# Two buffers for each load, three for the gate and x1 + b2, and new orders and banks in a batched graph-attention kernel

## The reference

```python
x = layernorm(x + elu(A(x)))           # layer A: one head, width 256
h = elu(B(x) + b1)                     # layer B: 4 heads of width 128
x = layernorm(x + C(h) + b2)           # layer C: one head, width 256, input width 512
# a layer: V = in @ W; e = leaky_relu(V a1 + (V a2)^T, 0.2), masked by adj;
#          out = softmax(e) @ V
# A masks by adj (softmax over columns), B and C by adj or the diagonal (over rows)
```

## Time and profile before

| | us |
|---|---|
| median of 3 runs | 724.78 (724.01 to 726.85) |
| the profiled execution | 722.46 |
| its span, first to last instruction | 720.7 |
| PE busy | 650.2 (90%) |
| DVE busy | 603.4 (84%) |
| ACT busy | 484.5 (67%) |
| POOL busy | 450.3 (62%) |
| mean granted TensorE clock, share of full | 0.972 |

### The profile page before, as it was taken

The page is one execution under the profiler, slowest core; times in us unless marked ns, Lnnn a source line. Parts: engine busy times, 40 slices in busy tenths (PEclk is TensorE's granted clock), DMA queues, the critical chain, the costliest instruction groups (busy, mean ns, idle before and its releaser), DMA issues. The chain is left out here.

```text
span 720.7 us, 17574 instructions
## 1 busy us (share of the span) xinstructions
PE 650.2 (90%) x4104; PEld 569.4 (79%) x4104; DVE 603.4 (84%) x2368; ACT 484.5 (67%) x1219; POOL 450.3 (62%) x810
## 2 busy tenths in 40 slices
PE   2478999999999999999899999999999999999883
PEld 1367788888888888888788888888888888888772
DVE  3566789989988989988889999899999889888862
ACT  1245777776777777787677776777777777777551
POOL 0215666766667766766667666666677666666752
PEclk9588999999999999999999999999999999999996
DMA  7211112322232213222232223222222123222111
GB/s 216 68 38 59 53 40 95 97 89 67 96 97 95 71 64 97 96 89 67 96 96 81 68 82 96 88 69 96 96 96 89 62 79 94 71 88 67 53 37 44
DMA packets 56085, 58.41 MB, mean 81 GB/s; under 512 B 3760, under 2 KB 51504, under 8 KB 55984
## 3 DMA queue, kind: packets, MB, share of 16 engines
q1 hardware_dynamic: 53152, 55.06, 23.7%
q10 hardware_dynamic: 2832, 2.23, 1.0%
HBM read 36.31 MB, written 8.39 MB: 62 GB/s over the span
## 5 line engine op out<-in xcount | busy, mean ns | idle before, releaser
L346 POOL TENSOR_SCALAR probB<-probB,rdenB 128x256 f32<-128x256 f32 x256 | 119.2, 478 | 101.9 <-DVE rdenB L654 97.8
L428 ACT ACTIVATE probB<-probB,shiftB 128x256 f32<-128x256 f32 x256 | 127.4, 500 | 66.8 <-DVE probB L637 54.1
L873 PE MATMUL PS<-probTB,VB 128*128 128x256 f32 x512 | 126.9, 389 | 0.0
L637 DVE SCALAR_TENSOR_TENSOR probB<-PS,VB,gatedB 128x256 f32<-128x256 f32 x256 | 110.6, 474 | 0.3 <-issue 0.2
L873 PEld LDWEIGHTS PS<-probTB,VB 128*128 128x128 f32 x512 | 91.1, 193 | 17.3 <-ACT probTB L439 8.5
L357 POOL TENSOR_TENSOR inlC<-hidT,inhC 128x512 fp32r<-128x512 f32 x64 | 82.1, 1283 | 24.7 <-ACT inhC L484 24.7
L595 DVE CUSTOM_DVE_ANT_0 gatedB<-PS,gateB 128x256 f32<-128x256 f32 x256 | 93.6, 421 | 2.8 <-issue 0.3
L814 PE MATMUL PS<-WA,xTin 128*128 128x258 f32 x256 | 65.8, 401 | 21.4 <-DMA xTin<-in_x_t_dram 21.2
L329 POOL TENSOR_TENSOR y<-y,xres 128x512 f32<-128x512 f32 x32 | 41.0, 1282 | 69.7 <-DVE y L659 69.7
L829 PE MATMUL PS<-WhB,inhB 128*128 128x260 f32 x256 | 78.2, 305 | 7.0 <-DVE inlB L668 7.0
L829 PE MATMUL PS<-WhC,inhC 128*128 128x258 f32 x256 | 78.1, 305 | 1.0 <-ACT VA L418 1.0
(11 more groups left out here) (98 smaller groups left out, 1651.4 us busy)
## 6 DMA issues: line engine op xcount, KB each, us to landing
adj_in<-in_adj_dram SPq DMA_DIRECT2D x32, 256.0 KB, 3.0
xTin<-in_x_t_dram SPq DMA_DIRECT2D x32, 256.0 KB, 3.7
xres<-in_x_dram SPq DMA_DIRECT2D x32, 256.0 KB, 3.2
adjT_in<-in_adj_t_dram SPq DMA_DIRECT2D x32, 256.0 KB, 2.9
x1c<-x1b SPq DMA_DIRECT2D x32, 256.0 KB, 2.3
out_dram<-res SPq DMA_DIRECT2D x32, 256.0 KB, 2.1
gateC<-gateB SPq DMA_DIRECT2D x32, 128.0 KB, 2.0
WB<-in_L_gnn_W_dram ACTq DMA_DIRECT2D x2, 256.0 KB, 5.8
```

The costliest lines, as they stand in the source:

```text
L346: last = pool.tensor_scalar(B.prob[h][:, k, :], B.prob[h][:, k, :], B.rden[:, k, h:h + 1], 1.0, ALU.mult, ALU.mult)
L428: last = nc.scalar.activation(L.prob[h][:, k, :], L.prob[h][:, k, :], ACT.Exp, bias=L.shift[:, k, h:h + 1], accum_out=den[:, k, h:h + 1] i ...
L637: last = nc.vector.scalar_tensor_tensor(out=L.prob[h][:, k, :], in0=PS[b][:, (h % 2) * N:(h % 2 + 1) * N], scalar=L.V[:, k, h, 1:2], in1=L ...
L873: last = nc.tensor.matmul(PS[b][:, o:o + N], B.V[:, k, h, 2:B.F + 2], B.probT[h][:, k, :], start=(k == 0), stop=(k == NT - 1))
```

## The change

- xTin, xres, adj_in and adjT_in have two buffers and two semaphores each. Batch b uses buffer b % 2, and its load waits for the reader of batch b - 2. All four are issued an iteration ahead of before, in the order residual, transposed adjacency, xT, adjacency, store.
- gate_to_c and x1_to_c are gone. Gate B/C and x1b have three buffers (b % 3), read in place by B and C; make_gate_b waits for the maxima of B and C of batch b - 3, keep_x1 for norm_last of batch b - 3.
- Each engine's list has a new order, over batches t0 to t5 (37 iterations; the first only issues loads). PSUM banks are dealt out anew: the eight-bank table is replaced by a record, kept while the program is built, of what last ended in a bank (take_bank).

The arithmetic is the same. The core of the diff (removed orders stand in the kernel above):

```diff
+    def loaded(self):
+        return (self.at // 2 + 1) * DMA
...
+        xTin = [sb(f"xTin{i}", [P, A.KT, N]) for i in range(2)]
...
+        gate_bc = [sb(f"gate_bc{i}", [P, NT, N], BF16) for i in range(3)]
...
+        x1b = [sb(f"x1b{i}", [P, NT, D]) for i in range(3)]
...
-            for i in range(NB + 4):
+            for i in range(NB + 5):
...
             def load_residual(t):
                 if active(t):
-                    if t.later:
-                        sp.wait_ge(s_t0, t.last())
-                    sp.dma_start(xres[:, :, :], x_v[t.at]).then_inc(s_xr, DMA)
+                    if t.at >= 2:
+                        sp.wait_ge(s_t0, t.this() - 2)
+                    sp.dma_start(xres[t.at % 2][:, :, :], x_v[t.at]).then_inc(s_xr[t.at % 2], DMA)
...
             def body(i):      # sync queue
+                load_residual(t0)
+                load_adjT(t1)
+                load_xT(t0)
+                load_adj(t0)
+                store(t5)
...
             def body(i):      # GpSimd
+                low_c(1, t4)
+                low_c(0, t4)
+                scale(2, t3)
+                scale(3, t3)
+                residual(t2)
+                scale(0, t3)
+                rstd(A, t2)
+                normalise(A, t2)
+                diagonal(t2)
+                fix_scores(t4)
+                scale(1, t3)
+                rstd(C, t5)
+                normalise(C, t5)
+                keep_x1(t2)
...
             def body(i):      # ScalarE
+                high_b(5, t3)
+                elu_exp(1, 0, t4)
+                exp(A, 0, t2)
+                exp(C, 0, t5)
+                weights_copy(B, 1, 2, t4)
+                weights_copy(A, 0, 7, t2)
+                high_c(1, t4)
+                elu_exp(0, 6, t4)
+                weights_copy(C, 0, 3, t5)
+                high_c(0, t4)
+                exp(B, 2, t3)
+                norm_first(1, 3, t2)
+                exp(B, 3, t3)
+                norm_first(0, 5, t2)
+                elu_exp_first(t2)
+                values(A, 1, 7, t1)
+                values(A, 0, 1, t1)
+                exp(B, 0, t3)
+                values(C, 1, 7, t4)
+                weights_copy(B, 2, 3, t3)
+                values(C, 0, 1, t4)
+                exp(B, 1, t3)
+                weights_copy(B, 3, 3, t3)
+                weights_copy(B, 0, 2, t3)
...
             def body(i):      # VectorE
+                make_gate_a(t1)
+                maxima(B, 2, 1, t3)
+                maxima(B, 3, 1, t3)
+                logit(B, 2, 1, t3)
+                elu(0, 6, t4)
+                top(B, 1, t3)
+                values_b(1, 0, 2, t3)
+                shift(B, 1, t3)
+                values_b(0, 0, 0, t3)
+                inverse_sum(A, 1, 3, t2)
+                logit(B, 3, 1, t3)
+                inverse_sum(A, 0, 5, t2)
+                inverse_sum_head(2, t3)
+                maxima(B, 0, 4, t3)
+                maxima(B, 1, 4, t3)
+                inverse_sum_head(3, t3)
+                top(B, 0, t3)
+                logit(B, 0, 4, t3)
+                inverse_sum(C, 1, 2, t5)
+                elu_first(t2)
+                shift(B, 0, t3)
+                norm_last(1, 2, t5)
+                logit(B, 1, 4, t3)
+                inverse_sum_head(0, t3)
+                stats(A, t2)
+                meanvar(A, t2)
+                inverse_sum(C, 0, 0, t5)
+                norm_last(0, 0, t5)
+                maxima(A, 0, 6, t1)
+                stats(C, t5)
+                logit(A, 0, 6, t1)
+                top(A, 0, t1)
+                maxima(C, 0, 4, t4)
+                top(C, 0, t4)
+                meanvar(C, t5)
+                shift(C, 0, t4)
+                shift(A, 0, t1)
+                inverse_sum_head(1, t3)
+                low_b(5, t2)
+                make_gate_b(t1)
+                logit(C, 0, 4, t4)
+                values_b(0, 1, 5, t2)
+                values_b(1, 1, 1, t2)
+                elu(1, 0, t3)
...
             def body(i):      # TensorE
+                project(B, 0, 1, 5, t3)
+                project(B, 1, 1, 1, t3)
+                transpose_weights(B, 1, 2, t4)
+                transpose_weights(A, 0, 7, t2)
+                spread(B, 1, 1, t3)
+                transpose_weights(C, 0, 3, t5)
+                weigh_head(1, 6, t4)
+                project(B, 1, 0, 2, t3)
+                project(B, 0, 0, 0, t3)
+                weigh(A, 1, 3, t2)
+                weigh(A, 0, 5, t2)
+                spread(B, 0, 4, t3)
+                weigh(C, 1, 2, t5)
+                project_a(1, 7, t1)
+                project_a(0, 1, t1)
+                weigh(C, 0, 0, t5)
+                transpose_weights(B, 2, 3, t3)
+                spread(A, 0, 6, t1)
+                project(C, 1, 0, 7, t4)
+                project(C, 0, 0, 1, t4)
+                transpose_weights(B, 3, 3, t3)
+                transpose_weights(B, 0, 2, t3)
+                spread(C, 0, 4, t4)
+                weigh_head(2, 0, t3)
+                transpose_x1(5, t2)
+                weigh_head(3, 0, t3)
+                weigh_head(0, 6, t3)
```

More of the change, by code:

```diff
@@ L327, in residual @@
                     pool.wait_ge(s_y0, t.this())
-                    pool.wait_ge(s_xr, t.this(DMA))
-                    pool.tensor_tensor(y0[:, :, :], y0[:, :, :], xres[:, :, :], ALU.add).then_inc(s_t0, 1)
+                    pool.wait_ge(s_xr[t.at % 2], t.loaded())
+                    pool.tensor_tensor(y0[:, :, :], y0[:, :, :], xres[t.at % 2][:, :, :], ALU.add).then_inc(s_t0, 1)
             def keep_x1(t):
@@ L335, in keep_x1 @@
                     pool.wait_ge(A.s_ln, t.this())
-                    if t.later:
-                        pool.wait_ge(s_x2c, t.last(DMA))
-                    pool.tensor_tensor(x1b[:, :, :], x1[:, :, :], b2p[:, :].unsqueeze(1).to_broadcast([P, NT, D]),
-                                       ALU.add).then_inc(s_x1b, 1)
+                    if t.at >= 3:
+                        for s in C.s_norm:
+                            pool.wait_ge(s, t.this() - 3)
+                    pool.tensor_tensor(x1b[t.at % 3][:, :, :], x1[:, :, :],
+                                       b2p[:, :].unsqueeze(1).to_broadcast([P, NT, D]), ALU.add).then_inc(s_x1b, 1)
             def scale(h, t):
@@ L370, in body @@
             def body(i):
-                t0, t1, t2, t3, t4 = i.batch(0), i.batch(1), i.batch(2), i.batch(3), i.batch(4)
-                residual(t0)
-                scale(3, t1)
-                scale(0, t1)
-                scale(1, t1)
-                rstd(A, t0)
-                fix_scores(t2)
-                keep_x1(t1)
-                normalise(A, t0)
-                rstd(C, t3)
-                normalise(C, t3)
-                diagonal(t0)
-                low_c(1, t1)
-                low_c(0, t1)
-                scale(2, t0)
+                t0, t1, t2, t3, t4, t5 = i.batch(0), i.batch(1), i.batch(2), i.batch(3), i.batch(4), i.batch(5)
+                low_c(1, t4)
[12 more added lines that the diff above has]
+                keep_x1(t2)
             iterations(body)
@@ L698, in norm_last @@
                     dve.wait_ge(C.s_den[u], t.this())
-                    dve.wait_ge(s_x2c, t.this(DMA))
+                    dve.wait_ge(s_x1b, t.this())
                     if t.later:
@@ L729, in body @@
             def body(i):
-                t0, t1, t2, t3, t4 = i.batch(0), i.batch(1), i.batch(2), i.batch(3), i.batch(4)
-                maxima(B, 2, 0, t2)
-                maxima(B, 3, 0, t2)
-                logit(B, 2, 0, t2)
-                top(B, 1, t2)
-                values_b(1, 0, 5, t2)
-                if t2.first:
-                    finish_b2(5)
-                shift(B, 1, t2)
-                inverse_sum(A, 1, 1, t1)
-                logit(B, 3, 0, t2)
-                gate_a(t0)
@@ L742, in body @@
-                inverse_sum(A, 0, 3, t1)
-                inverse_sum_head(2, t2)
-                maxima(B, 0, 6, t2)
-                maxima(B, 1, 6, t2)
-                top(B, 0, t2)
-                if t1.first:
-                    split_weights(B)
-                elu_first(t1)
-                shift(B, 0, t2)
-                logit(B, 0, 6, t2)
-                inverse_sum_head(3, t2)
-                logit(B, 1, 6, t2)
-                inverse_sum(C, 1, 1, t4)
-                inverse_sum_head(0, t2)
@@ L756, in body @@
-                inverse_sum(C, 0, 5, t4)
-                norm_last(1, 1, t4)
-                norm_last(0, 5, t4)
-                inverse_sum_head(1, t2)
-                stats(A, t1)
-                meanvar(A, t1)
-                if t1.first:
-                    score_columns(C, (0,))
-                stats(C, t4)
-                maxima(A, 0, 2, t0)
-                maxima(C, 0, 0, t3)
-                top(A, 0, t0)
-                logit(A, 0, 2, t0)
-                if t0.first:
+                t0, t1, t2, t3, t4, t5 = i.batch(0), i.batch(1), i.batch(2), i.batch(3), i.batch(4), i.batch(5)
```

(5 more changed lines are left out.)

208 lines of the change are left out of this document (55 added, 153 removed).

## The result

The changed kernel takes 680.44 us (median of 4 runs, 679.14 to 680.93) against 724.39 us for the kernel before in the same comparison (723.01 to 726.85). The ratio is 0.9387, with a 95% interval of 0.9358 to 0.9416: 44 us less. The profiled execution has a span of 679.2 us.

What follows compares the result with a forecast made beforehand. TensorE was taken as the bound, VectorE close behind. Steady turn 19.27 + 0.1 + 0.13 = 19.5 us; 37.5 + 26 + 20 + 565.5 + 44.8 = 693.8 span, forecast 696 us, range 684 to 708, 682 to 715 with most of the first rival.

Steps and rivals of the forecast that it cites:

- The load's wait: TensorE's project_a waiting for xTin: goes with two buffers per load, -9.6 us over 29 turns (bounds -9.6 to 0).
- No DMA copies: Two DMAs a turn (gateC, x1c) leave the sync queue: worth nothing alone, since no engine waits for them.
- The two covers, 0.36 and 0.46: TensorE's waits a turn before the projection (0.36) and the x1 transposes (0.46): both covered by other work in the new order.
- VectorE: VectorE's turn: 17.58 work, 0.97 idle and 0.4 for held gates make 18.95 us, 0.3 below TensorE's 19.27.
- The seams: TensorE's remaining idle time between groups: stays at 0.57 us a turn, giving a floor of 18.7 + 0.57 = 19.27.
- 0.1 for banks: TensorE groups waiting for a copy out of a PSUM bank: 0.1 us a turn added, bounds 0 to 0.8.
- 0.13 for late gates: Turns in which a held VectorE gate reaches low_b: 0.13 us a turn added.
- turns near 19.0: Steady turns near 19.0 us, total below 682 us; chance 0.03.
- The ramps: Start and end of the span: first mark 37.5, second 26 (bounds 23 to 28), third 20, tail 44.8 us.
- only the load's wait goes: First rival: TensorE's other idle time returns under other names, turn stays 20.09; 715 us, with ramps 709 to 719; chance 0.18.
- The second: Rival: VectorE gates, tops and shifts held by GpSimd become the bound, turn 21.5, 755 us; chance 0.09.
- The third: Rival: sync queue stands at the residual, gate B waits for its adjacency by 1 us or more, 721 to 728; chance 0.03.

Runs made afterwards that it cites:

- experiment 1: Kernel before, still one xTin buffer, with xT's load moved ahead of the store in the sync queue: 718.13 us, ratio 0.9912.
- experiment 8: Changed kernel with one buffer for each of the four loads and the residual loaded one batch later: 679.06 us, ratio 0.9385.
- experiment 2: Kernel before with keep_x1 behind layer A's normalise, three x1b buffers read in place and x1's DMA copy removed: 732.13 us, ratio 1.0121.
- experiment 11: Changed kernel with the x1 transposes one head's product later on TensorE: 707.56 us, ratio 0.9743.
- experiment 10: Changed kernel with GpSimd's keep_x1 ahead of layer A's normalise, as in the old order: 720.31 us, ratio 0.9936.
- experiment 9: Changed kernel with ScalarE's exp(A) ahead of the high half of x1, as in the old order: 718.19 us, ratio 0.9896.
- experiment 3: Kernel before with the edits of experiment 1 and experiment 2, and the x1 transposes one head's product earlier: 710.38 us, ratio 0.9821.
- experiment 12: Changed kernel with one more VectorE statistics instruction a turn, ahead of layer A's ELU: 690.58 us, ratio 0.9514.
- experiment 6: The kernel of experiment 5 with x1's transposes in bank 3 instead of bank 2: 688.51 us, ratio 0.9505.
- experiment 4: The kernel of experiment 3 with ScalarE's high half of x1 ahead of exp(A): 701.28 us, ratio 0.9661.
- experiment 7: The kernel of experiment 4 with x1's transposes in bank 3 instead of bank 2: 698.82 us, ratio 0.9649.
- experiment 14: Changed kernel with xT and adjacency loaded first and the second batch's loads held until the first projection: 677.97 us, ratio 0.9335.
- experiment 5: The kernel of experiment 4 with VectorE's tops and shifts of layers A and C ahead of their logits: 709.3 us, ratio 0.9797.

## Why the prediction was too high, step by step

**The load's wait: right that it goes, wrong in what it was worth.** The cause is the queue place alone (experiments 1 and 8). The 9.6 was the mean turn over the undisturbed one, and all of it was put down to the load. Experiment 1 takes every such wait away and gains 5.5; the rest lies in turns that are long for other reasons. The change has such turns too (seven of 19.17 to 19.58), 2.3 us in all, so of the 9.6 it gets 7.3.

**No DMA copies: not tried alone.** Experiment 2 takes x1's copy away but moves keep_x1 as well. Gates read in place were in every new kernel and in no old one. "No engine waits for them in a steady turn" holds for the trace before, where GpSimd's two waits for x1's copy, 1.2 us, lie behind 660 us. It doesn't hold once the queue is changed: in experiment 1 one such wait made a turn 1.84 longer. Beyond that the zero in the sum stands untested.

**The two covers, 0.36 and 0.46: they hold, with a condition missing.** The chain x1 transposes to projection is 349.95 - 347.77 = 2.18 now, and it is filled to 0.02. Experiment 11 takes the first one away and pays 27 us, 1.0 a turn for 0.86 of cover. Experiment 10 pays 40 us for keep_x1's old place, but there another chain comes last, so the cover of the normalising is shown by its room alone, 0.33 where I had 1. But the sum lacked the condition on which the first one stands: the high half must not stand behind exp(A). The change makes that move, I costed it at nothing, and experiment 9 puts 38 us on it. I read the wait of low_b in the earlier trace rows as a matter of TensorE's order alone; experiment 3 shows that in the old order both covers together leave the turn at 20.08. That the gain of the order came out no smaller than forecast is luck in this respect: the change makes the missing move without the sum asking for it.

**VectorE: the turn about right, the ranking wrong.** Forecast 18.95, 0.3 below TensorE. Its list takes 19.05 and starts low_b without idle time, and experiment 12 charges the full 0.35. Its busy time is 18.21 against a forecast of 17.98 (17.58 + 0.4), although gate A lost only about 0.16 in most turns and top(A) fell to 0.21 (0.16 forecast); its waits are 0.84 against 0.97. The 0.23 more of work is spread thin, and I did not find it in one row.

**The seams: the step that failed.** "The seams stay, 0.57", with 0.1 for banks and 0.13 for late gates on top, made 19.5 out of 18.7 of work. The undisturbed turn is 19.06 and the mean 19.14. So the seams are 0.36 where the sum had 0.57, and the two additions are 0.08 (mean over undisturbed turn) where it had 0.23. 29 x 0.21 = 6.1 and 29 x 0.15 = 4.4 make the 10.5 us, 29 x (19.5 - 19.14), of the 14.6 by which the span (693.8 forecast, 679.2 measured) was missed. The mistake was to carry what was left after two named waits over to another order as a fixed cost. The earlier trace rows could have shown it otherwise: the four products at 327.17 are followed 0.86 later by the transposes, 4 x 0.215, with no seam at all. By the starts, part of the 0.57 was waits at groups whose copy was just late. The clearest one, ScalarE and TensorE of the kernel before:

```profile
312.05 0.58 ACT L439 ACTIVATE probTA<-PS 128x512 f32<-128x512 f32 x1
```

```profile
312.49 0.28 PE L829 MATMUL PS<-WhB,inlB 128*128 128x260 f32 x1
312.77 1.97 PE L862 MATMUL PS<-VA,probTA 128*128 128x257 f32 x8
```

and TensorE of the kernel after, where that copy is through 2.4 us earlier:

```profile
336.35 0.28 PE L801 MATMUL PS<-WhB,inlB 128*128 128x260 f32 x1
336.51 2.00 PE L834 MATMUL PS<-VA,probTA 128*128 128x257 f32 x8
```

The rounded record lasts 0.12 to the next start: 0.28 - 0.12 = 0.16 lost before, 0.04 after. Around project_a and C's weighing 0.13 became 0.05. But 0.09 between layer A's weighing and the spread behind it did not go, it is 0.12 after. And in experiment 6 the old order, without either named wait, still stands 0.64 above its work. So the seams did not shrink with the repairs; they belong to the order, and the new list has fewer late copies. The split is read from starts; no run takes one seam away. I had the case "turns near 19.0" on the list and gave it 0.03, too little for a kernel whose new list moves every group. So the failed step is a term that was mis-sized: the two named waits went, as the sum had it, and what was to stay was smaller.

**The ramps: 4.0 us, three of four terms too high.** The first mark was forecast at 37.5 and came at 37.9: 1.4 to 1.6 later at the loads, where I had 1.3, so the transposes' new bank gave about what was forecast, 1.2. Experiments 4 and 7 differ by that bank, and their first marks by 1.6. The second mark took 24.05 (forecast 26, bounds 23 to 28), the third 18.67 (forecast 20), the tail 43.64 (forecast 44.8). I had left them longer than the turn for no wait that I could name. 1.95 + 1.33 + 1.16 - 0.4 = 4.0, and with 10.5 this is the 14.6 to a rounding. What hides in the second mark was not tested; experiments 8, 9 and 14 have it 0.8 to 0.9 shorter than the change.

**The rivals.** The first, "only the load's wait goes", is out in the new order, and it is very nearly what experiment 1 measured in the old one: 718. The second, holds on VectorE making it slower, is out as a whole: gate A pays 0.16 in most turns. Its case did come true once, with 1.34 for gate A in the turn of 19.58. The third is out: the residual's load is issued at 343.78 and xT's at 344.76, and nothing waits for either.

```profile
344.76 0.41 SPq L204 DMA_DIRECT2D xTin<-in_x_t_dram  x1
```

**The Trainium skill's rule on the shared port** ("SBUF — State Buffer", Who interferes with whom) was weighed for top(A), and the row was followed against it. That row was misread. The normalising is two instructions of 0.55 us from 325.46, and shift(A) at 325.98 fell on the boundary between them. Well inside one of the two a shift is held as well. Experiment 6, VectorE and GpSimd:

```profile
291.18 0.41 DVE L626 SCALAR_TENSOR_TENSOR shiftC<-topC,amaxC 128x2 f32<-128x2 f32 x1
```

```profile
290.48 1.10 POOL L320 TENSOR_SCALAR x<-y,nmA,rstdA 128x256 f32<-128x256 f32 x2
```

Both end near 291.58, and nearly every turn of experiments 5 and 6 has such a shift(C). So the traces agree with the rule, for one-input GpSimd operations too. It cost the forecast nothing: top(A), 0.11 behind the start of the diagonal, takes 0.21, some 0.05 more than the 0.16 alone.

## What to carry to other kernels

Count the engine's own work from its start-to-start times, and take every microsecond above it for a wait until a row shows otherwise; what is left over after the named waits belongs to the order it was measured in and is not a constant. The mean turn less the undisturbed one is a sum of causes too, not the price of the one that has a name. When engines run hand-ordered lists in lockstep, follow the whole chain around the seam of a turn through every engine, with what stands ahead of each step in its list and its bank: a repair of one chain alone moves the work to the next, and can cost time (experiments 2 and 5), while the last of a set seems worth everything (21 us for a bank, 38 for one line). Before doubling a buffer, look where its load stands in the queue.

## What the runs showed of the hardware

Groups of different kinds on TensorE (128-column transposes, 256-column f32 products, rounded products) follow one another without loss: 0.02 us over five changes. The exception seen is the first rounded record of a group: 330.90 to 331.10, and 342.84 to 343.04, 0.20 to the next record where the others take 0.12.

A VectorE operation on two columns can take 1.19 us when a two-input GpSimd operation runs beside it, and 0.41 inside one of a one-input GpSimd operation's instructions (experiment 6), against 0.12 to 0.16 alone; both times it ends with the GpSimd instruction. What matters is where it hangs: in experiment 3 it holds up ScalarE, in experiment 4 only VectorE.

A gate, one input of 512 columns, takes 0.42 us with GpSimd idle. For gate B beside the normalising in the kernel before, the start decides: where it starts 0.01 to 0.13 us behind the normalising it takes 0.42 or 0.43, and the normalising 1.33 or 1.34 instead of 1.25; where it starts 0.16 to 0.29 us behind, it takes 0.55 to 0.68 and the normalising 1.25. So the 0.64 and the 0.43 of the earlier trace rows are both gates beside the normalising, at different starts. Gate A, started 0.22 us inside keep_x1, took 1.34.
